# Gate rows of two of four experts rebuilt on the chip from three bf16 parts

## The reference

```python
x = x + conv(ln_c(x), Wc, bc)              # relu(cosine similarity)^2 between all pixels of an image
t = to_tokens(x)
u = ln_t(t)
# gates: graph attention (4 heads x 4 experts), layer norm, mean over heads
topk_s, topk_i = jax.lax.top_k(scores, 2)
w = jax.nn.softmax(topk_s, axis=-1)
for ei in range(4):
    g = jnp.where(topk_i == ei, w, 0.0).sum(-1)
    hh = jax.nn.gelu(u @ W1[ei] + b1[ei], approximate=False)     # 64 -> 128
    out = out + g[..., None] * (hh @ W2[ei] + b2[ei])            # 128 -> 64
x = from_tokens(t + out)
```

## Time and profile before

| | us |
|---|---|
| median of 3 runs (5215.01 to 5220.03) | 5218.09 |
| the profiled execution's own time | 5217.17 |
| its span, first to last instruction | 5214.9 |
| VectorE busy in the span | 3969.3 (76%) |
| TensorE (products) | 3470.7 (67%) |
| ScalarE | 3405.7 (65%) |
| GpSimd | 2917.5 (56%) |
| largest item on SP's queue: `gs<-gates_d` | 64 transfers of 1152 KB |

### The profile page before, as it was taken

One profiled execution on the slowest core, in us unless ns is written; L12 is line 12 of the kernel. 1 busy time (PEld: TensorE's weight loads), 2 busy tenths in 40 slices (PEclk: granted clock), 3 DMA queues, 4 the chain that ended last, 5 costly groups with the idle time before them and its releaser, 6 DMA issues.

```text
span 5214.9 us, 70585 instructions
## 1 busy us (share of the span) xinstructions
PE 3470.7 (67%) x22687; PEld 1460.3 (28%) x22687; DVE 3969.3 (76%) x5512; ACT 3405.7 (65%) x4010; POOL 2917.5 (56%) x2937
## 2 busy tenths in 40 slices
PE   4888988600399999999999999940000017777777
PEld 1223333200144444444444444420000002222222
DVE  8998988997767767777767665635888948778777
ACT  4787978500587877787778777733555527666666
POOL 6000000048777777777777777777774147666661
PEclk9898999855699999999999999975555558899999
DMA  6100110002122222222222222233545526999997
GB/s 256 42 20 21 25 29 16 13 18 83 21 44 56 53 52 55 56 54 52 60 51 53 60 51 51 53 59 116 177 166 195 171 73 144 150 156 165 160 156 153
DMA packets 322231, 441.88 MB, mean 85 GB/s; under 512 B 185241, under 2 KB 251676, under 8 KB 321260
## 3 DMA queue, kind: packets, MB, share of 16 engines
q1 hardware_dynamic: 199504, 288.13, 21.1%
q0 software_dynamic: 105536, 148.61, 16.8%
q10 hardware_dynamic: 16896, 1.18, 0.2%
HBM read 252.35 MB, written 166.47 MB: 80 GB/s over the span
## 4 chain that ended last, share of the span: by engine, by line
POOL 39%; issue 14%; DMA 13%; DVE 10%; SPq 1%; PE 1%; ACT 0%; DVEq 0%; POOLq 0%; ACTq 0%
POOL rows L984 35%; DMA rows<-htab_d,idx 6%; DMA gs<-gates_d 5%; POOL R L1769 2%; DVE ms L2641 1%; DVE pairs L2648 1%; DVE S L2519 1%; SPq L1680 1%; DVE AD L2504 1%; DVE AE L2498 1%; POOL nb L1726 1%; DVE total L2650 0%; POOL got L1724 0%; PE ye L1941 0%; POOL raw_d L963 0%
## 5 line engine op out<-in xcount | busy, mean ns | idle before, releaser
L984 POOL DMA_INDIRECT rows<-htab_d,idx x2048 | 2093.9, 1022 | 663.8 <-issue 606.5
L2073 ACT ACTIVATE rel<-gram 128x1024 f32<-128x1024 f32 (+1 forms) x1080 | 1003.1, 933 | 350.5 <-PE gram L1885 344.1
L2418 DVE SCALAR_TENSOR_TENSOR s<-gram,rel 128x1024 f32<-128x1024 f32 (+1 forms) x720 | 793.3, 1117 | 559.9 <-ACT rel L2073 543.3
L1839 PE MATMUL acc<-s,gT 128*64 128x512 f32 (+1 forms) x4320 | 1031.4, 554 | 0.4 <-issue 0.4
L1885 PE MATMUL gram<-hl 128*64 128x512 f16 (+1 forms) x4320 | 798.2, 366 | 108.9 <-DVE s L2418 65.4
L1885 PE MATMUL gram<-hl,lh 128*64 128x512 f16 (+1 forms) x4320 | 788.1, 362 | 0.0
L1769 POOL DMA_INDIRECT R<-seg_d,nidx x576 | 591.0, 1026 | 194.2 <-issue 168.8
L1084 POOL IOTA slots<- 64x2048 int32 x1 | 1.8, 1832 | 974.1 <-POOLq L192 974.1
L1941 PE MATMUL ye<-hid,w 128*64 128x384 f32 x1536 | 353.7, 538 | 285.4 <-DVE ms L2641 166.5
L2165 ACT ACTIVATE hid<-up,b1t 128x768 f32<-128x768 f32 x384 | 335.7, 899 | 254.2 <-PE up L1953 226.2
L1924 PE MATMUL tailsT<-ident,tails 128*20 128x128 f32 x24 | 5.2, 412 | 731.2 <-DVE tails L2527 731.2
(11 more groups left out here) (372 smaller groups left out, 5404.8 us busy)
## 6 DMA issues: line engine op xcount, KB each, us to landing
gs<-gates_d SPq DMA_DIRECT2D x64, 1152.0 KB
rows<-htab_d,idx POOLq DMA_INDIRECT x2048
seg_d<-state SPq DMA_DIRECT2D x32, 996.0 KB, 4.2
raw_d<-w_zeros POOLq DMA_DIRECT2D x48, 512.0 KB, 23.2
raw_d<-rows POOLq DMA_DIRECT2D x32, 768.0 KB
tne<-tn_d SPq DMA_DIRECT2D x64, 288.0 KB
x2e<-x_d SPq DMA_DIRECT2D x64, 288.0 KB
out<-res SPq DMA_DIRECT2D x64, 288.0 KB, 8.4
```

What stands on the lines that cost most here:

```text
L984: pool.indirect_dma_start(out=n.rows[:, k % 2, j, :], out_offset=None, in_=n.htabx, in_offset=bass.IndirectOffsetOnAxis(ap=n.idx[:, g % 2, ...
L1839: last = pe.matmul(acc[(par + c) % 2][j * C:(j + 1) * C, 0:w], gT[:, par, 2 * k + j, :], s2[:, u % SLOTS, j * w:(j + 1) * w], start=k == 0 ...
L2073: act.activation(rel[:, t % RELS, 0:2 * w].rearrange("p (j x) -> p j x", j=2), gram[(par + t) % 2][:, :, 0:w], ACT.Relu, scale=1.0 / SPLIT ...
L2418: dve.scalar_tensor_tensor(halves(s2[:, t % SLOTS, 0:2 * w]), gram[(par + t) % 2][:, :, 0:w], 1.0 / SPLIT ** 2, halves(rel[:, t % RELS, 0: ...
```

## The change

In `GH` the four rows of an image stay as they are. Experts 0 and 1 go the old way, through `gates_d` (now two rows) and the repeating load. For experts 2 and 3 VectorE takes the upper 16 bits of each float32 as a bf16 number, subtracts it (`GR`), and does so once more (`GL`); the upper halves of the three are a bf16 sum that equals the float32 number. ScalarE copies these three parts into `GP` (128 x 6 x 18) and stores them to `parts_d`, a second store of each image on its queue. SP loads them to three partitions of each half (`gw`, 3 x 2 x 1152 bf16). For each step with `k >= 2` TensorE multiplies the three rows with ones (`ones3`, 3 x 64), which adds the parts and repeats the row on 64 partitions, into a PSUM buffer `gp` (two of one bank); ScalarE copies this to `gs` after the next step's Gelu (`copied`). To make room in PSUM the first layer has two buffers `up` instead of three, so `up(i)` waits for the Gelu of `i - 2`. VectorE's product waits for the copy (`a_gs`) where `k >= 2`, and TensorE waits for the gate loads (`gl_in`) at step 2. In the first image the gates' store of the next one moves from step 8 to 7.

```diff
-    n.gates = nc.dram_tensor("gates_d", (NX, M), F32).ap()
+    n.gates = nc.dram_tensor("gates_d", (NX // 2, M), F32).ap()
+    n.parts = nc.dram_tensor("parts_d", (PARTS * NX // 2, M), BF16).ap()
...
-        up = [late.enter_context(nc.psum_tensor(f"up{i}", [P, 2, 512], F32)) for i in range(GROUP)]
+        up = [late.enter_context(nc.psum_tensor(f"up{i}", [P, 2, 512], F32)) for i in range(2)]
+        gp = [late.enter_context(nc.psum_tensor(f"gp{i}", [P, 512], F32)) for i in range(2)]
...
             def load_gates(b, par, nth):
-                sp.wait_ge(g_out[par], 16 * (nth + 1))
+                sp.wait_ge(g_out[par], 32 * (nth + 1))
...
-                spread = lambda a, z: rows_of[:, a:z].rearrange("e (a x) -> a e x", a=1).to_broadcast((C, NX, z - a))
+                spread = lambda a, z: rows_of[:, a:z].rearrange("e (a x) -> a e x", a=1).to_broadcast((C, NX // 2, z - a))
...
                 for h in range(2):
-                    sp.dma_start(gs[h * C:(h + 1) * C, par], spread(h * HALF, (h + 1) * HALF)).then_inc(gl_in[par], 16)
+                    sp.dma_start(gs[h * C:(h + 1) * C, par, 0:NX // 2], spread(h * HALF, (h + 1) * HALF)).then_inc(gl_in[par], 16)
+                    sp.dma_start(gw[h * 32:h * 32 + PARTS, par, :, :], parts_of[:, :, h * HALF:(h + 1) * HALF]).then_inc(gl_in[par], 16)
...
             def combine(b, par, nth, before, ahead):
...
-                    if before or i >= GROUP:
-                        pe.wait_ge(a_hid, b * ESTEPS + i + 1 - GROUP)
+                    if before or i >= 2:
+                        pe.wait_ge(a_hid, b * ESTEPS + i - 1)
...
+                    if k >= NX // 2:
+                        if i == NX // 2:
+                            pe.wait_ge(gl_in[par], 64 * (nth + 1))
+                        at_least(pe, a_gs, (b * ECH + cp) * (NX // 2) + k - NX + 1)
+                        for h in (0, 1):
+                            pe.matmul(gp[k % 2][h * C:(h + 1) * C, 0:EW], ones3[h * 32:h * 32 + PARTS, :],
+                                      gw[h * 32:h * 32 + PARTS, par, k - NX // 2, cp * EW:(cp + 1) * EW], start=True, stop=True)
                     if i >= 2:
                         down(b, i - 2, not before)
...
+            def copied(par, i):
+                cp, k = divmod(i, NX)
+                if k >= NX // 2:
+                    act.activation(gs[:, par, k, cp * EW:(cp + 1) * EW], gp[k % 2][:, 0:EW], ACT.Copy).then_inc(a_gs, 1)
...
+            def gates_out(k, par, nth):
                 act.wait_ge(v_gt, k + 1)
-                act.dma_start(one_of(gatev, k).rearrange("a p e t -> (a p) e t"), GH[:, par, :, :]).then_inc(g_out[par], 16)
+                act.dma_start(one_of(gatev, k).rearrange("a p e t -> (a p) e t"),
+                              GH[:, par, 0:TW * NX // 2].rearrange("p (e t) -> p e t", t=TW)).then_inc(g_out[par], 16)
...
+                for a, whole in enumerate((GH[:, par, TW * NX // 2:], GR[:, :], GL[:, :])):
+                    top = whole.bitcast(BF16)[:, 1::2].rearrange("p (e t) -> p e t", t=TW)
+                    last = act.activation(GP[:, par, a * (NX // 2):(a + 1) * (NX // 2), :], top, ACT.Copy)
+                last.then_inc(a_gx, 1)
+                act.wait_ge(a_gx, 4 * k + 4)
+                act.dma_start(one_of(partv, k).rearrange("a p r t -> (a p) r t"), GP[:, par, :, :]).then_inc(g_out[par], 16)
...
                     act.wait_ge(pe_up, b * ESTEPS + i + 1)
-                    act.activation(hid[:, i % GROUP, :, :], up[i % GROUP][:, :, 0:EW], ACT.Gelu, bias=b1t[:, i % NX:i % NX + 1]).then_inc(a_hid, 1)
+                    act.activation(hid[:, i % GROUP, :, :], up[i % 2][:, :, 0:EW], ACT.Gelu, bias=b1t[:, i % NX:i % NX + 1]).then_inc(a_hid, 1)
+                    if i >= 1:
+                        copied(par, i - 1)
+                    elif before:
+                        copied(1 - par, ESTEPS - 1)
...
+                    top = lambda t: t.bitcast(BF16)[:, 1::2]
+                    late_half = GH[:, par, TW * NX // 2:]
+                    link(dve.tensor_tensor(GH[:, par, :].rearrange("p (e t) -> p t e", t=TW), U1[:, :, :], b4(s4[:, :]), ALU.mult))
+                    link(dve.tensor_tensor(GR[:, :], late_half, top(late_half), ALU.subtract))
+                    dve.tensor_tensor(GL[:, :], GR[:, :], top(GR[:, :]), ALU.subtract).then_inc(v_gt, 1)
...
                 dve.wait_ge(pe_y, b * ESTEPS + i + 1)
+                if k >= NX // 2:
+                    dve.wait_ge(a_gs, (b * ECH + cp) * (NX // 2) + k - NX // 2 + 1)
```

More of the change, by code:

```diff
@@ L29 @@
 IN_FLIGHT = 4
+PARTS = 3
 EARLY = 10
@@ L1397, in flow @@
         xs = ph("xs", [P, TW, NX])
-        GH = ph("GH", [P, 2, NX, TW])
+        GH = ph("GH", [P, 2, NX * TW])
+        GR = ph("GR", [P, TW * NX // 2])
+        GL = ph("GL", [P, TW * NX // 2])
+        GP = ph("GP", [P, 2, PARTS * NX // 2, TW], BF16)
+        ones3 = ph("ones3", [NX // 2 * 16 + PARTS, C], BF16)
         tne = ph("tne", [P, 2, HALF])
@@ L1421, in flow @@
         gs = ph("gs", [P, 2, NX, HALF])
+        gw = ph("gw", [NX // 2 * 16 + PARTS, 2, NX // 2, HALF], BF16)
         ms = ph("ms", [P, 2, NX, EW])
@@ L1491, in flow @@
         pe_y = sem("pe_y")
+        a_gs = sem("a_gs")
         a_hid = sem("a_hid")
@@ L1554, in flow @@
         gatev = n.gates.rearrange("e (b p t) -> b p e t", p=P, t=TW)
+        partv = n.parts.rearrange("r (b p t) -> b p r t", p=P, t=TW)
         def one_of(view, b):
@@ L1682, in load_gates @@
             def load_gates(b, par, nth):
-                sp.wait_ge(g_out[par], 16 * (nth + 1))
+                sp.wait_ge(g_out[par], 32 * (nth + 1))
                 sp.sem_inc(sp_passed, 1)
                 rows_of = n.gates[:, bass.ds(b * NP, NP)] if not isinstance(b, int) else n.gates[:, b * NP:(b + 1) * NP]
-                spread = lambda a, z: rows_of[:, a:z].rearrange("e (a x) -> a e x", a=1).to_broadcast((C, NX, z - a))
+                spread = lambda a, z: rows_of[:, a:z].rearrange("e (a x) -> a e x", a=1).to_broadcast((C, NX // 2, z - a))
+                parts_of = n.parts[:, bass.ds(b * NP, NP)] if not isinstance(b, int) else n.parts[:, b * NP:(b + 1) * NP]
+                parts_of = parts_of.rearrange("(a k) x -> a k x", a=PARTS)
                 for h in range(2):
-                    sp.dma_start(gs[h * C:(h + 1) * C, par], spread(h * HALF, (h + 1) * HALF)).then_inc(gl_in[par], 16)
+                    sp.dma_start(gs[h * C:(h + 1) * C, par, 0:NX // 2], spread(h * HALF, (h + 1) * HALF)).then_inc(gl_in[par], 16)
+                    sp.dma_start(gw[h * 32:h * 32 + PARTS, par, :, :], parts_of[:, :, h * HALF:(h + 1) * HALF]).then_inc(gl_in[par], 16)
             def store_out(b, par):
@@ L1948, in combine @@
                         pe.wait_ge(tx_in[par], 64 * (nth + 1))
[L1949 to L1950 removed]
+                    if before or i >= 2:
+                        pe.wait_ge(a_hid, b * ESTEPS + i - 1)
                     for h in (0, 1):
                         rows_ = slice(h * C, (h + 1) * C)
[L1953 removed]
+                        last = pe.matmul(up[i % 2][:, h, 0:EW], w1[rows_, k, :], tne[rows_, par, cp * EW:(cp + 1) * EW], start=True, stop=True)
                     last.then_inc(pe_up, 1)
+                    if k >= NX // 2:
[5 more added lines that the diff above has]
+                                      gw[h * 32:h * 32 + PARTS, par, k - NX // 2, cp * EW:(cp + 1) * EW], start=True, stop=True)
                     if i >= 2:
@@ L2152, in weights_of @@
                 act.activation(es[:, :, :], xs[:, :, :], ACT.Exp).then_inc(a_gx, 1)
-            def gates_out(k, par):
-                act.wait_ge(v_gt, k + 1)
-                act.dma_start(one_of(gatev, k).rearrange("a p e t -> (a p) e t"), GH[:, par, :, :]).then_inc(g_out[par], 16)
+            def copied(par, i):
[3 more added lines that the diff above has]
+            def gates_out(k, par, nth):
+                act.wait_ge(v_gt, k + 1)
+                act.dma_start(one_of(gatev, k).rearrange("a p e t -> (a p) e t"),
+                              GH[:, par, 0:TW * NX // 2].rearrange("p (e t) -> p e t", t=TW)).then_inc(g_out[par], 16)
+                if not isinstance(nth, int) or nth:
+                    act.wait_ge(g_out[par], 32 * nth)
+                for a, whole in enumerate((GH[:, par, TW * NX // 2:], GR[:, :], GL[:, :])):
[4 more added lines that the diff above has]
+                act.dma_start(one_of(partv, k).rearrange("a p r t -> (a p) r t"), GP[:, par, :, :]).then_inc(g_out[par], 16)
             own_of(0)
@@ L2159, in _ @@
             weights_of(0)
-            gates_out(0, 0)
+            gates_out(0, 0, 0)
             def combine(b, par, nth, before, ahead):
@@ L2181, in combine @@
                     if ahead >= 2 and i == OUT_AT:
-                        gates_out(b + 2, par)
+                        gates_out(b + 2, par, nth + 1)
             mix(act, combine)
+            act.wait_ge(pe_y, B * ESTEPS - 1)
+            copied(1, ESTEPS - 1)
         @block.vector
```

(1 more changed line is left out.)

26 lines of the change are left out of this document (12 added, 14 removed).

## The result

The changed kernel takes 5240.17 us (median of 6 runs, 5236.30 to 5244.93) beside 5215.44 for the kernel before (6 runs, 5208.35 to 5220.03): ratio 1.0049, 95% interval 1.0036 to 1.0062. The forecast was 5192, a gain. The profiled execution has a span of 5236.4 us (its own time 5238.27), 21.5 more than before.

What follows compares the result with a forecast made beforehand. VectorE's 25.0 us per image plus 4.2 of gate-row stalls bound the kernel; afterwards 25.5 + 1.7 + 0.4 = 27.6. Winning 39 us, losing 6 at each end and about 2 at first gates: net 25, 5192 us; 8 in 10: 5138 to 5245.

Steps and rivals of the forecast that it cites:

- wait (2): TensorE's step 3 needs Gelu 1, behind an Exp and two table loads: 0 to 1.2 us, taken as 0.4 per image.
- (1): VectorE waits once per image for ScalarE's copy of expert 3, behind the gate store: 1.0 to 2.3 us, mean 1.7.
- The split itself: Two added subtractions of 128x36 per image on VectorE, 0.5 us, raising its 25.0 us per image to 25.5.
- the queue's 29.3 us become about 21.6: On SP's queue, 1.15 MB less per image at 149 GB/s saves 7.7 us, putting it below VectorE's 25.0.
- the copy: ScalarE's copy of 128x384 out of PSUM, six per image: 0.49 us each.
- the pair: TensorE's two products with ones, six pairs per image: 0.35 us each, 2.1 us per image.
- the wait for its own part copies: ScalarE waits for its part copies before the second gate store: 0.15 us, an estimate.
- the other two table switches: Other places where two `up` buffers might make TensorE wait for Gelu; it was said to be ahead there.
- rival D: ScalarE's copies between Gelus need table loads: 15.4 us per image, some 430 us slower; chance 0.02.
- C's mechanism: Gate rows land late by their own stores, with twice the packets on ScalarE's queue: slower, 5259 us; chance 0.18.
- B's mechanism: Two `up` buffers cost 0.4 us at all three table switches, 28.4 us per image: a wash, 5214 us; chance 0.18.
- The rule of turns: A DMA engine takes turns between queues, one packet at a time; cited for 174 packets per us alone, 49 beside loads.

Runs made afterwards that it cites:

- e9: The kernel before with two `up` buffers instead of three and half the gathers: 26.00 us per image, ratio 0.9758 to the kernel before.
- e13: The changed kernel with half the gathers, without pairs with ones and copies; split and second store stay: 27.90 us per image, ratio 0.9919 to the kernel before.
- e6: The changed kernel with 9 of the 18 gathers of `R` per image: 29.30 us per image, ratio 1.0005 to the kernel before.
- e7: The changed kernel with three `up` buffers, no pairs with ones, no copies, and half the gathers: 26.49 us per image, ratio 0.9834 to the kernel before.
- e15: The changed kernel with copies behind their own Gelus, gate store and first Exp later, half the gathers: 25.92 us per image, ratio 0.9823 to the kernel before.
- e5: The kernel before with 9 of the 18 gathers of `R` per image: 25.22 us per image, 5089.6 us, ratio 0.9761 to the kernel before.
- e3: The changed kernel with three `up` buffers, no pairs with ones, no copies, all gathers: 29.29 us per image, 5228.3 us, ratio 1.0007 to the kernel before.
- e14: The changed kernel, nothing left out, with copies behind their own Gelus, gate store and first Exp later: 28.96 us per image, ratio 1.0005 to the kernel before.

## Why the prediction was wrong

*The step that failed in the sum: wait (2), "two `up` buffers 0.4 us".* It was priced as one step late once: step 3, behind Gelu 1, at most 1.2 us of TensorE. Measured are stands of 2.24 us at step 3 in one image and of 2.50 at step 2 in the next, for Gelu 0, which (2) did not look at; 1.94 us of VectorE's waits for `ye`; and 29.13 us per image for 27.6. (29.13 - 27.6) x 23 = 35 us, and (29.5 - 27.6) x 5 = 9 us more in the first images, which had no stall to give back: 44 of the 48 us by which 5192 missed 5240. Two buffers alone are nearly as cheap as said (0.78, e9). What was not seen is that they meet the longer store of the gate rows (2.68 together, e13), and the pairs and copies behind it (29.30, e6): ScalarE's stand, reckoned only as a late copy in (1), also empties TensorE, which then stands up to 2.5 us and at times returns at granted 0.53. The split itself was charged 0.5, for the subtractions; with three buffers it cost 1.27 (e7). Moving that store, with the copies behind their own Gelus, takes most of the price away (25.92 us per image, e15).

*A second step was wrong, and hidden by the first: "the queue's 29.3 us become about 21.6".* The 149 GB/s were the rate of SP's queue beside the gathers, not a rate of its own; e5 moves the full bytes at 172 GB/s. The view of the earlier trace rows had the sign in it: q0 with 43.9% of the engines' time for 3.07 MB beside 59.62. What SP's queue gave up went for the most part to the gathers (43.9% to 52.3%, 59.0% in e14). With (2) right the change would still have stayed near 29 us (e3, e14), and the forecast of a gain would still have failed.

*Right:* `gs` transfers of half the size (576 KB); no VectorE stall on the gate loads; the copy 0.48 us (0.49 forecast), the pair 0.35, the two subtractions 0.48 (0.5); the wait for its own part copies 0.15, as estimated; TensorE ahead, or 0.20 us late as a rule, at the other two table switches; 6.5 us lost behind image 28 (6). Not one of the 138 copies from 4474 to 5148 has a table load, so rival D did not come. The Trainium skill ("ScalarE: Activation LUTs", Table sets: the hidden batching unit) says that copy sits in every set, and this trace agrees. The wait for copies, 1.63 (1.7), is right as a sum and in part by luck: it comes 39 times in 23.5 images and not once in each.

C's mechanism did not occur: from 4474 to 5148 `gates_d` lands after 4.4 to 10.1 us, 5.6 in the middle (12.3 in the earlier trace rows), and `parts_d` after 8.8 in the middle, 12.5 at most. So its time, 5259, came nearest for another reason. The rate that C took for its packets "alone" was measured beside gathers: q0 fills the engines in that window (101.4% by the profile, 4742 to 4745). B's mechanism, two buffers late, comes nearest to the one seen, at 29.1 us instead of 28.4, but the long stands lie at the store and the first switch, not at all three.

*What stays open:* why a gather's packet takes 0.05 or 0.5 us. With SP's queue empty in both, the changed kernel has this from 4394 to 4398 and then from 4454 to 4458:

```profile
q0 software_dynamic: 96, 0.04, 8.1%
...
q0 software_dynamic: 109, 0.04, 88.7%
```

That is 0.054 and 0.52 us each at about the same number and bytes. So their number per us alone does not decide it, as the first images of the kernel before show too. The rule of turns that the prediction cited from the Trainium skill ("DMA: Bandwidth & Descriptors", Queues, rings and completion order) is not the reason either: in the slow stretch no other queue moved a packet. What makes a packet dear, and why half the gathers stay cheap, no run here shows.

## What to carry to other kernels

A DMA share of 0.99 and a queue's GB/s don't say that this queue's bytes are the limit: divide each queue's share by its packets, and take away another queue's work once, before bytes are saved. A buffer taken from a ring is to be priced at the longest stand of its consumer, not at the usual step, and a store that waits for another engine belongs where that engine has long finished.

## What was not expected of the hardware

Half of the gathers per image, 57% of the packets per us, cut their share of the DMA engines from 43.9% to 8.6%. In the first images all 18 gathers had only 9.1%, at no fewer packets per us. A stand of TensorE of 2.50 us was followed by some 4 us at granted 0.53, so this one cost 1.55 us more than itself; others of that length were not followed so at once. In e15, whose longest stand for Gelu was 1.0 us, the clock was 1.00 for 500 us, at 0.85 of the time busy.
